# Sixteen groups instead of twelve beside the deform tiles of a four-layer convolution kernel, and two groups sampled in their own pass

## What is computed

```python
off = offset.reshape(Bx, KK, 2, Hx, Wx)          # 9 offsets a pixel, from a convolution of x and 8 cosines
y0, x0 = floor(py), floor(px)
g00, g01, g10, g11 = gather(y0, x0), gather(y0, x0 + 1), gather(y0 + 1, x0), gather(y0 + 1, x0 + 1)
val = (g00 * (1 - wy1) * (1 - wx1) + g01 * (1 - wy1) * wx1 + g10 * wy1 * (1 - wx1) + g11 * wy1 * wx1) * mask
out = einsum('bckhw,ock->bohw', val, weight)     # and the layer's input is added (residual)
```

## Time and profile before

| | us |
|---|---|
| median of 3 runs (8682.15 to 8694.11) | 8690.26 |
| the profiled execution's own time | 8690.2 |
| its span, first to last instruction | 8688.5 |
| DVE busy in the span | 5470.7 |
| POOL busy in the span | 5373.3 |
| PE busy in the span | 5125.1 |
| ACT busy in the span | 2522.5 |

### The profile page before, as it was taken

How to read it: one execution, slowest core, us unless ns; L and a number is a source line. 1 busy time by engine, 2 the same in 40 slices (tenths; PEclk the granted TensorE clock), 3 DMA queues, 4 the chain that set the end, 5 groups by cost and what they waited for, 6 DMA issues and landing times. The chain is left out here.

```text
span 8688.5 us, 87034 instructions
## 1 busy us (share of the span) xinstructions
PE 5125.1 (59%) x26946; PEld 3335.9 (38%) x26946; DVE 5470.7 (63%) x6302; ACT 2522.5 (29%) x4248; POOL 5373.3 (62%) x5206
## 2 busy tenths in 40 slices
PE   4556676767767666767767667677766732222222
PEld 3333324544444435544444335444444411111111
DVE  5688556668873565678864666688854654444444
ACT  1355331235432312245522312255502300000000
POOL 0000005768877657768877657778877667777776
PEclk9877888888878878878888878888888865555555
DMA  2000023333333543333333533423343533333333
GB/s 79 22 0 0 22 85 110 111 111 90 91 115 113 163 140 104 111 106 90 92 122 110 170 126 112 125 87 91 90 127 115 168 110 113 113 113 113 113 112 104
DMA packets 443201, 887.62 MB, mean 102 GB/s; under 512 B 119072, under 2 KB 268918, under 8 KB 439924
## 3 DMA queue, kind: packets, MB, share of 16 engines
q0 software_dynamic: 248832, 679.81, 26.8%
q1 hardware_dynamic: 190708, 129.65, 5.3%
q10 hardware_dynamic: 3456, 75.50, 2.1%
HBM read 763.04 MB, written 121.53 MB: 102 GB/s over the span
## 5 line engine op out<-in xcount | busy, mean ns | idle before, releaser
L657 POOL DMA_INDIRECT gathered_corners<-gather_table,metas x5184 | 5365.0, 1035 | 3294.2 <-issue 2902.3
L1364 PE MATMUL ps<-ident,weighted_corners 128*128 128x128 f32 (+1 forms) x7680 | 1211.7, 328 | 1086.0 <-DVE weighted_corners L726 1085.4
L1364 PEld LDWEIGHTS ps<-ident,weighted_corners 128*128 128x128 f32 (+1 forms) x7680 | 1095.7, 166 | 1266.2 <-issue 780.2
L726 DVE TENSOR_TENSOR weighted_corners<-gathered_corners,ps 128x2304 f32<-128x2304 f32 x384 | 980.8, 2554 | 738.1 <-DMA gathered_corners<-gather_table,metas 622.6
L1124 ACT COPY sampled_by_channel<-ps 128x512 f32<-128x512 f32 x576 | 335.2, 582 | 3509.1 <-PE ps L1364 1832.8
L1444 PE MATMUL ps<-region,woff 128*128 (+2 forms) x3456 | 1237.5, 517 | 23.3 <-ACT region L1109 23.3
L1367 PE MATMUL ps<-ident,sampled 128*128 128x128 f32 (+1 forms) x960 | 232.9, 402 | 1430.1 <-DVE sampled L745 1267.0
L1444 PEld LDWEIGHTS ps<-region,woff 128*128 128x128 f32 x3456 | 692.6, 204 | 523.1 <-issue 102.5
L1367 PEld LDWEIGHTS ps<-ident,sampled 128*128 128x128 f32 (+1 forms) x960 | 156.0, 195 | 1502.1 <-issue 1351.8
L1351 PE MATMUL ps<-sampled_by_channel,w 128*64 128x256 f32 x2880 | 619.6, 425 | 0.0
L739 DVE TENSOR_TENSOR ps<-gathered_corners,ps 128x1152 f32<-128x1152 f32 x144 | 196.2, 1362 | 645.5 <-DMA gathered_corners<-gather_table,metas 644.3
(11 more groups left out here) (222 smaller groups left out, 7722.6 us busy)
## 6 DMA issues: line engine op xcount, KB each, us to landing
gathered_corners<-gather_table,metas POOLq DMA_INDIRECT x5184
x_after_layer<-region ACTq DMA_DIRECT2D x8, 4608.0 KB, 12.4
gather_table<-tabst SPq DMA_DIRECT2D x192, 192.0 KB
region<-in_x_dram ACTq DMA_DIRECT2D x12, 1536.0 KB, 10.8
region<-x_after_layer ACTq DMA_DIRECT2D x4, 4608.0 KB, 14.8
res<-x_after_layer SPq DMA_DIRECT2D x144, 128.0 KB
out_dram<-ob SPq DMA_DIRECT2D x144, 128.0 KB
indices_and_weights<-region SPq DMA_DIRECT2D x16, 810.0 KB
```

Of the source, the lines that this page charges most:

```text
L657: pool.indirect_dma_start(out=G[:, s % NG, k, :], out_offset=None, in_=table, in_offset=bass.IndirectOffsetOnAxis(ap=idx[:, s * KK + k:s * ...
L726: ins = ch.after().tensor_tensor(W[:].rearrange("p q (k c) -> p q k c", c=C), Gq, w4, ALU.mult)
L1364: mm = pe.matmul(out_m, W[:, q, 128 * m:min(128 * m + 128, KK * C)], ident[:, :], start=q == 0, stop=q == 3, is_transpose=True)
```

## The change

The groups are handed out anew. The twelve deform tiles hold sixteen groups: three tiles hold four groups, with five, five and six steps in their six places. The convolution of layer 1 and layer 2 (sums and products together) hold two groups each in place of four each. DVE's and ACT's loops over the tiles are unrolled by three, PE's fully. The product that fetches a tile's largest offset (`max_tr`) moves to a later place.

The 36 slots of a pass no longer take the 36 groups of the pair before. Slots 0 to 33 (`OWN = 34`) take its groups 2 to 35. The last two slots, in the offsets stage, take groups 0 and 1 of the pair being prepared, whose weights SP copies straight from SBUF (`take_meta`) once the first part of `meta` is made; pass 0 has these two slots too, and pass 4 has 34 slots. At the end of a pass SP also copies the weights of group 2 into the first slot, so that the next pass starts without `load_meta(0, 0)`.

```diff
+TRIPLE = 3
+TAP_GROUPS = 4
+G_TAPS = (G_NORM + 1, G_NORM + 1 + 2 * TAP_GROUPS)
+G_CONV = (G_TAPS[1] + 2 * TAP_GROUPS, G_TAPS[1] + 2 * TAP_GROUPS + 2)
+G_COSINES = G_CONV[1] + 2
+OWN_GROUPS = 2
+OWN = GROUPS - OWN_GROUPS
+def triple_places():
+    steps = iter([(m, s) for m in range(TAP_GROUPS) for s in range(STEPS)])
+    return [[(next(steps),) if at < count else () for at in range(6)] for count in (5, 5, 6)]
-CONV_PLACES = ((0,), (1, 2), (3,))
+CONV_PLACES = ((0,), (), (1,), (2,), (), (3,))
-SUM_PLACES = ((0,), (), (), (1,), (), (), (2,), (), (3,), (), (), ())
+SUM_PLACES = [[(2 * j + e // 6,) if e % 6 == 0 else () for e in range(12)] for j in range(2)]
...
+                def take_meta(group, slot):
+                    sp.dma_start(metas[:, slot, :], meta_all[:, group * META:(group + 1) * META]).then_inc(meta_loaded[slot], 16)
...
                 for q in range(PAIRS):
                     load_cosines(q, q % 2)
+                    if q == 5:
+                        sp.wait_ge(meta_made, 1)
+                        sp.wait_ge(x3_stored, 16)
+                        sp.wait_ge(tab_put[0], 16 * RT + 32 + 16)
+                        sp.wait_ge(tab_put[1], 16 * RT + 32)
+                        sp.wait_ge(weighted, (OWN - 1) * STEPS + CREDIT)
+                        take_meta(0, OWN % 2)
...
+                sp.wait_ge(weighted, (OWN + 1) * STEPS + CREDIT)
+                take_meta(OWN_GROUPS, 0)
...
-                with pool.Fori(0, GROUPS // 2) as j:
+                with pool.Fori(0 if sample else OWN // 2, GROUPS // 2 if prepare else OWN // 2) as j:
...
-                            if at == 2:
+                            if at == MAX_PLACE[u] + 1:
                                 v.wait_ge(max_tr, t + 1)
...
-                            for gi, s in PLACES[tiles_groups[e]][at]:
-                                steps_of(j + G_TAPS[e], (j + G_TAPS[e]) % 2, (s,))
+                            for m, s in PLACES[u][at] if sample else ():
+                                steps_of(j * TAP_GROUPS + (G_TAPS[e] + m), (G_TAPS[e] + m) % 2, (s,))
```

More of the change, by code:

```diff
@@ L495, in program @@
                 metap = meta_dram[bass.ds(p * 128, 128), :]
+                out_now = xout[bass.ds(p * 128, 128), :]
             if sample:
@@ L528, in _ @@
                 if sample:
-                    load_meta(0, 0)
                     group(0, 0, first=True)
                     group(1, 1)
-                    ahead = G_COSINES if prepare else GROUPS - 2
+                    ahead = G_COSINES if prepare else OWN - 2
                     with sp.Fori(1, ahead // 2) as j:
@@ L536, in _ @@
                 if not prepare:
[L537 to L540, removed]
+                    group(OWN - 2, 0)
+                    group(OWN - 1, 1, last=True)
+                    store_out(OWN - 1)
+                    sp.wait_ge(out_stored, 16 * (OWN + 1))
                     return
@@ L619, in _ @@
                     load_cosines(q, q % 2)
[L620 to L632, removed]
-                store_meta(PARTS - 2)
-                if sample:
-                    store_out(GROUPS - 1)
-                    sp.wait_ge(out_stored, 16 * (GROUPS + 1))
+                    if q == 5:
[5 more added lines that the diff above has]
+                        take_meta(0, OWN % 2)
+                        if sample:
+                            store_out(OWN - 2)
+                            load_res(OWN - 1)
+                        store_meta(0)
+                    if q == 9:
+                        sp.wait_ge(weighted, OWN * STEPS + CREDIT)
+                        take_meta(1, (OWN + 1) % 2)
+                    if q == 10:
+                        if sample:
+                            store_out(OWN - 1)
+                        load_res(OWN)
+                        store_meta(1)
+                store_out(OWN)
+                load_res(OWN + 1)
+                store_meta(PARTS - 2)
+                sp.wait_ge(weighted, (OWN + 1) * STEPS + CREDIT)
+                take_meta(OWN_GROUPS, 0)
+                store_out(OWN + 1)
+                sp.wait_ge(out_stored, 16 * (GROUPS + 1))
+                sp.wait_ge(meta_loaded[0], 16 * (GROUPS // 2 + 1))
                 store_meta(PARTS - 1)
@@ L756, in steps_of @@
                 def steps_of(g, slot, steps, sum_on_pe=True, first=False):
-                    if sample:
+                    if sample or (isinstance(g, int) and g >= OWN):
                         for s in steps:
@@ L769, in _ @@
                     v.sem_inc(s_, count)
+                if sample:
+                    v.sem_inc(meta_loaded[0], 16)
+                else:
+                    for s_, count in ((weighted, OWN * STEPS), (transposed, OWN * STEPS), (vt_copied, OWN * STEPS), (proj_done, 2 * OWN),
+                                      (group_added, OWN), (out_stored, 16 * OWN), (res_loaded, 16 * OWN),
+                                      (meta_loaded[0], 16 * (OWN // 2)), (meta_loaded[1], 16 * (OWN // 2))):
+                        v.sem_inc(s_, count)
                 if not prepare:
@@ L772, in _ @@
                     ch.restart()
-                    with v.Fori(1, GROUPS) as g:
+                    with v.Fori(1, OWN) as g:
                         steps_of(g, g % 2, (0, 1, 2, 3), False)
                         ch.restart()
-                    finish(GROUPS - 1)
+                    finish(OWN - 1)
                     ch.restart()
@@ L966, in _ @@
                 v.wait_ge(x1_back, 16)
-                for j in range(4):
-                    for e in range(3):
-                        q = j * 3 + e
+                for j in range(2):
+                    for e in range(6):
+                        q = j * 6 + e
                         steps_of(j + G_CONV[0], (j + G_CONV[0]) % 2, CONV_PLACES[e])
@@ L989, in _ @@
                 ch.restart()
-                with v.Fori(0, 2) as j:
+                for j in range(2):
                     for e in range(12):
-                        steps_of(j + G_CONV[1], (j + G_CONV[1]) % 2, SUM_PLACES[e])
+                        steps_of(G_CONV[1], G_CONV[1] % 2, SUM_PLACES[j][e])
                     ch.restart()
-                with v.Fori(0, 2) as j:
+                for j in range(2):
                     for e in range(12):
                         t = j * 12 + e
-                        steps_of(j + (G_CONV[1] + 2), (j + G_CONV[1]) % 2, SUM_PLACES[e])
+                        steps_of(G_CONV[1] + 1, (G_CONV[1] + 1) % 2, SUM_PLACES[j][e])
                         v.wait_ge(c2_mm, t + 1)
@@ L1091, in _ @@
                     for s in ((2, 3) if h == 0 else (0, 1, 2, 3)):
-                        steps_of(h + G_OFFSETS, (h + G_OFFSETS) % 2, (s,), False)
+                        steps_of(h + G_OFFSETS, (h + G_OFFSETS) % 2, (s,), False, first=not sample and h + G_OFFSETS == OWN)
                         for part, piece in META_PLACES.get((h, s), ()):
@@ L1133, in _ @@
                 if not prepare:
-                    with act.Fori(0, GROUPS) as g:
+                    with act.Fori(0, OWN) as g:
                         steps_of(g, range(STEPS))
@@ L1177, in _ @@
                 for e in range(2):
-                    with act.Fori(0, 6) as j:
-                        t = j + 6 * e
+                    with act.Fori(0, 2) as j:
+                      for u in range(TRIPLE):
+                        t = j * TRIPLE + (u + 6 * e)
                         def place(at):
-                            for gi, s in PLACES[tiles_groups[e]][at]:
-                                steps_of(j + G_TAPS[e], (s,))
+                            for m, s in PLACES[u][at] if sample else ():
+                                steps_of(j * TAP_GROUPS + (G_TAPS[e] + m), (s,))
                         off = ps[:, 0:4, 0:RN]
@@ L1242, in _ @@
                 act.dma_start(x_flat1, x1p).then_inc(x1_back, 16)
-                with act.Fori(0, 4) as j:
+                with act.Fori(0, 2) as j:
                     steps_of(j + G_CONV[0], range(STEPS))
@@ L1247, in _ @@
                 normalize_upper(pad1_2[:, 1:1 + HW, 1:1 + HW], rows(x_flat1), xn2_ready)
-                with act.Fori(0, 2) as j:
+                for j in range(2):
                     for e in range(12):
@@ L1256, in _ @@
                         ins.then_inc(c2_copied, 1)
-                        steps_of(j + G_CONV[1], SUM_PLACES[e])
-                with act.Fori(0, 2) as j:
-                    steps_of(j + (G_CONV[1] + 2), range(STEPS))
+                        steps_of(G_CONV[1], SUM_PLACES[j][e])
+                steps_of(G_CONV[1] + 1, range(STEPS))
                 root(4)
@@ L1381, in _ @@
                 if not prepare:
-                    with pe.Fori(0, GROUPS) as g:
+                    with pe.Fori(0, OWN) as g:
                         steps_of(g, range(STEPS), False)
@@ L1450, in offset_tile @@
                     for at in range(6):
-                        for gi, s in PLACES[tiles_groups[e]][at]:
```

(16 more changed lines are left out.)

40 lines of the change are left out of this document (20 added, 20 removed).

## The result

The changed kernel takes 8745.6 us (median of 4 runs, 8743.4 to 8754.4) against 8692.2 for the one before: a ratio of 1.0065, 95% interval 1.0049 to 1.0081. It is slower, by 53.4 us between the medians; 8716, 26 us more than before, was forecast. The profiled execution has a span of 8744.7 us, 56.2 more than before.

A forecast was written before the change was run, and what follows sets the result against it. POOL's gathers were taken to bound the deform tiles, with DVE full too. From 8690.2 us, +47 (pass 0), +72 (passes 1 to 3, +24 each) and -93 (pass 4) gave 8716 us, range 8560 to 8845.

The forecast's parts named there:

- The deform tiles: Passes 1 to 3: four more groups at POOL's price, 180.0 us, 5.5 more loss, savings of 7 and 8: +171.
- my lower value: Deform tiles: the loss simply goes with the two-input instructions' time and stays at 10.7 us a tile.
- The correction for a thinner share: Deform tiles: two-input instructions fill 0.56 instead of 0.69, so 48 gathers lose 11.5 us a tile; 11.1 was taken.
- the two savings: Deform tiles: -7 us from a shorter stall in the first tile, -8 from the last step moving to place 5.
- Convolution and layer 2: Passes 1 to 3: with half the groups, convolution, sums and products take 240 us for 384.7: -145.
- The hand-over: Passes 1 to 3: +1 us for SP's wait before the cosines, -3 at a pass's start.
- Pass 4: Last pass, sampling only: two groups of 45.0 us fewer and 3 us off its start: -93.
- Pass 0: First pass: it gets two groups, +46 us, and 1 for the added reset: +47.
- B': Second rival for the faster side: DVE was the bound; deform tiles +37, a pass -110, total 8314 us; chance 0.08.
- B: Rival, deform tiles: loss falls to 7 us a tile, stage +121, a pass -26, total 8566 us; chance 0.12.
- C: Rival, deform tiles: each gather keeps its loss of 0.295 us; +207, a pass +60, total 8824; chance 0.12.
- D: Rival, convolution and layer 2: they give back only -103 us; a pass +66, total 8842; chance 0.10.

The follow-up runs named there:

- the PSUM run: Kernel before, with DVE's products and sums in the deform rounds reading PSUM in place of their second SBUF operand: 8650.2 us (one run).
- the added sums: Changed kernel with five DVE sums of two SBUF inputs added behind each step in pass 4, results unused: 8952.7 us (one run).

## Why the prediction was right, and where it was not

The direction and the range held, and so did the mechanism. The size did not: 26 us more were forecast, and 53 (medians) to 56 (profiled spans) came, twice as much.

*What bounds the kernel.* Right. POOL was last in the deform tiles, DVE close behind (668.6 against 684.4 us, by the PSUM run). The second rival for the faster side, that DVE was the bound, asked for +37 us in the deform tiles and gave way to their +164; the PSUM run, which shortens the stage without shortening DVE's work by more than 3 us, speaks against it as well.

*The deform tiles*, +171 forecast, +164.4 measured. The loss (the time by which gathers are longer than 0.944 us) was put at 133.5 us; 575 gathers of 1.162 lose 0.217 each, 125. It was 128 before: the loss goes with the time of DVE's two-input instructions, which did not change, as my lower value said (10.7 a tile; 10.4 measured), and hardly with the share that they fill. The correction for a thinner share was not needed. The Trainium skill's "SBUF — State Buffer" ("Who interferes with whom") has it that a DVE instruction with two SBUF inputs contends with a GpSimd instruction that reads SBUF, and that the later comer waits. The traces agree for the gather, which waits until the DVE instruction ends. For DVE they don't: the 319 added sums that start 0.14 to 0.9 us into a gather take 0.957 to 0.959 us, as long as alone. One reading of mine was off: I took the stretched gather beside L926 for held by L926. By the timeline of the added sums it was L925, which ended at 2108.09, 0.83 us before the gather did. L925 reads two operands from SBUF as well, so the mechanism stands. Of the two savings, 7 and 8 us, the stall in the first tiles did shrink as forecast (13.5 to 6.4 us), but POOL's waits for DVE as a whole fell only from 14.1 to 10.8; the other has no run of its own, and the window holds 140 more gathers in place of 144.

*Convolution and layer 2*, -145 forecast, -138.2 measured: 113.1, 71.9 and 61.5 for 110, 73.5 and 56.5. The first two were paced by PE as said (100.2 of 113.1, 64.6 of 71.9 busy). The products miss by 5: PE was to hold DVE up by 5 us more than in pass 0, and DVE is idle for 20.2 of the 61.5 us, against 8.6 of 41.0 there, so by 11.6.

*The hand-over* was put at +1 and -3 us. Pass 1 grew by 26.4 us, of which the stages above explain 164.4 - 138.2 = 26.2, so all the rest of the pass comes to +0.2 for -2. Passes 1 to 3 came to +26, +21 and +24 for +24 each; the sum is hit so closely (+71.8 for +72) because -7 and +7 cancel, and that is luck. *Pass 4*, -89.8 for -93.

*Pass 0* is the term that was mis-sized: +74 for +47. The own groups cost the +46 forecast. The later `max_tr` and the unrolled loops I had written off as hidden by the gathers, and in pass 0's deform tiles there are none, so they were put at nothing without a reason. They cost 28.3 us: 22 go with the late product (the run with the early fetch), and 6 stay, whose cause is open. This term alone is 27 of the 30 us by which the forecast missed. A smaller slip: what the range leaves out (B' and half each of B, C and D) has a chance of 0.25, not some 0.2.

Rival B, a loss that falls below 10.4 us a tile, was closer than its chance says: 10.4 is where it stood. The time still came out above that of before, mostly by pass 0's 27 us and by the 7 us a pass that the stages behind gave back less than forecast.

## What to carry to other kernels

Before work is moved from one stage to another, ask of each engine how full it is in the stage that receives, issue gaps included: a stage can be full for two engines at once, and the one that no wait names sets the price. Look at the mean length of one instruction in a stage against another; 1.24 against 0.94 us was the clue in this case. And an edit whose cost is hidden by a cover costs its full price in every pass where the cover is absent.

## What the hardware showed

A GpSimd gather by index takes 0.95 us when nothing holds it. If it starts under a DVE instruction that reads two operands from SBUF, it is held until that ends and runs on for about 0.8 us more: 0.81 to 0.83 us behind each of the 332 held gathers' sums, 0.77 to 0.79 us behind masked copies in the kernel before. Five sums of 0.96 us beside nine gathers cost 1.56 us a step (212 / 136). The same sums with one operand in PSUM held no gather (3 us in all of pass 4).

DVE is hardly slowed in turn. Its products and sums take 0.95 to 0.96 us in pass 0, with no gather, and beside gathers. Only where it starts within some 0.05 us of a gather's start can it lose a little: 35 of the 680 added sums take 0.97 to 1.03 us, and all 35 start so. With the second operand in PSUM none of 680 does.
